# Storing the last unit of tokens before the third expert's weights are loaded, in a one-core cross-attention and mixture-of-experts kernel

## The reference

```python
x = x + xattn(layernorm(x), ctx, mask)          # tanh attention, then w_s * features + b_s
xn = layernorm(x)
probs = softmax(xn @ gate)                      # 4096 tokens, 8 experts
scores, token_idx = top_k(probs.T, k=512)
tok = xn[token_idx]
h = gelu(tok @ W1 + b1)
out_tok = h @ W2 + b2
routed = zeros.at[token_idx].add(out_tok * scores)
shared = gelu(xn @ Ws1 + bs1) @ Ws2 + bs2
x = x + routed + shared
```

## Time and profile before

| | us |
|---|---|
| median of 3 runs | 908.18 |
| lowest and highest run | 906.77, 911.2 |
| the profiled execution | 906.4 |
| its span in the profile | 904.6 |

### The profile page before, as it was taken

One profiled execution on the slowest core, in us unless ns is written; L12 is line 12 of the kernel. 1 busy time (PEld: TensorE's weight loads), 2 busy tenths in 40 slices (PEclk: granted clock), 3 DMA queues, 4 the chain that ended last, 5 costly groups with the idle time before them and its releaser, 6 DMA issues.

```text
span 904.6 us, 14092 instructions
## 1 busy us (share of the span) xinstructions
PE 802.1 (89%) x5355; PEld 471.2 (52%) x5355; DVE 710.8 (79%) x1412; ACT 767.4 (85%) x600; POOL 312.9 (35%) x563
## 2 busy tenths in 40 slices
PE   6865678579998999999999999999899899999995
PEld 4321123124443444445444464456676779999985
DVE  5799889897989699987979985976887577667640
ACT  4989999999999999999999999996653476676671
POOL 3301540705642008674004720070204134454423
PEclk9999999989999999999999999999999999999998
DMA  8000000000000000200000100003003345545512
GB/s 264 17 0 1 1 1 1 24 1 24 1 24 24 1 1 24 71 1 1 24 1 1 51 21 1 23 25 116 25 24 129 104 118 140 141 117 115 137 20 34
DMA packets 32405, 41.80 MB, mean 46 GB/s; under 512 B 2365, under 2 KB 29011, under 8 KB 32339
## 3 DMA queue, kind: packets, MB, share of 16 engines
q1 hardware_dynamic: 26083, 32.49, 10.9%
q0 software_dynamic: 6144, 8.39, 5.5%
q10 hardware_dynamic: 112, 0.04, 0.0%
HBM read 28.33 MB, written 12.58 MB: 45 GB/s over the span
## 4 chain that ended last, share of the span: by engine, by line
PE 38%; ACT 37%; issue 11%; DVE 9%; POOL 2%; DMA 1%; ACTq 0%; SPq 0%; DVEq 0%; POOLq 0%
ACT z L971 31%; PE bank L890 9%; PE bank L913 8%; PE bank L770 7%; PE bank L821 5%; DVE z L1329 4%; PE bank L806 3%; ACT z L967 2%; ACT u L1008 2%; PE bank L928 1%; PE bank L746 1%; PE bank L699 1%; DMA out_dram<-x_ring 1%; PE bank L864 1%; ACT L1008 1%
## 5 line engine op out<-in xcount | busy, mean ns | idle before, releaser
L971 ACT ACTIVATE z<-z 128x4096 f32<-128x4096 f32 (+5 forms) x157 | 521.1, 3365 | 6.2 <-DVE z L1329 6.0
L1329 DVE TENSOR_SCALAR z<-feat,txt_bias 128x1024 f32<-128x1024 f32 (+1 forms) x722 | 421.1, 654 | 34.6 <-PE bank L770 33.4
L770 PE MATMUL bank<-z,window 128*32 128x512 f32 x2464 | 307.2, 608 | 62.9 <-ACT z L971 61.4
L770 PEld LDWEIGHTS bank<-z,window 128*32 128x32 f32 x2464 | 70.1, 110 | 252.8 <-issue 136.0
L821 PE MATMUL bank<-ws_sb,u 128*128 128x256 f32 x512 | 128.1, 391 | 5.5 <-ACT u L1008 5.5
L821 PEld LDWEIGHTS bank<-ws_sb,u 128*128 128x128 f32 x512 | 93.2, 191 | 41.5 <-issue 19.8
L806 PE MATMUL bank<-tr,ws_s 128*128 128x512 f32 x384 | 107.4, 416 | 0.0
L890 PE MATMUL bank<-xg_s,w_s 128*128 128x512 f32 x384 | 101.0, 401 | 4.6 <-ACT hid L1044 4.4
L913 PEld LDWEIGHTS bank<-w_s,hid_s 128*128 128x128 f32 x672 | 86.4, 188 | 4.0
L913 PE MATMUL bank<-w_s,hid_s 128*128 128x256 f32 x672 | 88.2, 280 | 0.0
L806 PEld LDWEIGHTS bank<-tr,ws_s 128*128 128x128 f32 x384 | 69.5, 188 | 30.1 <-issue 16.4
(11 more groups left out here) (237 smaller groups left out, 750.9 us busy)
## 6 DMA issues: line engine op xcount, KB each, us to landing
w_raw<-in_L_ffn_W_dram SPq DMA_DIRECT2D x16, 1024.0 KB, 5.7
x_ring<-in_x_dram SPq DMA_DIRECT2D x8, 512.0 KB, 8.1
xn_dram<-xn SPq DMA_DIRECT2D x8, 512.0 KB, 2.9
out_dram<-x_ring SPq DMA_DIRECT2D x8, 512.0 KB, 2.9
u<-in_L_ffn_Ws_dram SPq DMA_DIRECT2D x1, 1024.0 KB, 11.2
ws_sb<-in_L_ffn_Ws_dram SPq DMA_DIRECT2D x1, 1024.0 KB, 13.6
xg<-xn_dram,idx POOLq DMA_INDIRECT x32, 4.0
out_dram<-y,idx POOLq DMA_INDIRECT x32, 3.9
```

What stands on the lines that cost most here:

```text
L770: ins = e.matmul(sums[v][32 * r:32 * r + 32, :], window[:, c, 31 - k:63 - k], z[:, n % ZB, at_piece:at_piece + TOK], start=(v, r) not in b ...
L971: e.activation(part, part, ACT.Tanh).then_inc(signal(*step), 1)
L1329: ins = e.tensor_scalar(z[:, n % ZB, i * width:(i + 1) * width], feat_of(units, c), bias_of(units, t, c), None, ALU.add)
```

## The change

Three settings change in the table of numbers at the top, and in `beside_experts` the place of the loads beside expert 0:

```diff
-EXPERT_FILL = (18, 5, 3)
+EXPERT_FILL = (20, 6, 0)
...
-LAST_END = 2
+LAST_END = 1
...
-        if ex + 2 < E and m in (1, 5):
-            steps.append(("load_w1" if m == 1 else "load_w2", ex + 2))
+        if ex + 2 < E and m in ((4, 7) if ex == 0 else (1, 5)):
+            steps.append(("load_w1" if m < 5 else "load_w2", ex + 2))
```

## The result

The changed kernel takes 900.81 us (median of 6 runs, 899.45 to 903.03), the kernel before 908.14 us (6 runs, 906.77 to 911.2). The ratio is 0.992, with a 95% interval from 0.9898 to 0.9942: 7.3 us faster, by the interval between 5.3 and 9.3 us. The profiled execution took 903.03 us, the slowest of the six, with a span of 901.3 us.

A forecast was written before the change was run, and what follows sets the result against it. The prediction took the late `x_ring` store, which stops ACT and then PE in expert 0, as the bound. 6.24 + 0.46 = 6.7 us off gave 899.7 us (profiled) or 901.5 us (median); forecast 901.0 us, range 898.8 to 903.8 us.

The forecast's parts named there:

- The wait and its cause: Expert 0: ACT's weight split waits 8.4 us for the `x_ring` store, held 7.6 us by its place in SP's queue.
- the distance: Time from expert 0's first `e_down` to expert 1's: 31.28 us before, 6.70 us longer than the next expert's 24.58 us.
- The sum, 6.24 + 0.46 = 6.7 us: Expert 0: 6.24 us for PE's stop plus 0.46 us for its list's wait on DVE's marking; bounds 6.2 and 8.2 us.
- 1.40 us of the 6.24 us are clock: After PE's 4.4 us idle, six matmuls took 2.93 us at half clock against 1.53 us at full clock.
- PE still had two slices in hand: At the store wait in expert 0, PE's loss is less than ACT's 8.4 us because two slices remained to work on.
- The down_end in a hole of DVE: Before slice 4's `e_lo`: the 1.28 us of `down_end` fill 0.96 us of DVE idleness, pushing `e_lo` some 0.3 us.
- EXPERT_FILL and the place of `load_w2` bring nothing: In expert 0: no shared-network matmul moves, and expert 2's `load_w2` still waits for the last `split_lo` of `w2`; no gain.
- The store's landing, 2.9 to 8.2 us, nearer to the first: SP's `x_ring` store, issued at about 705.6 us, lands at 708.5 us, at the worst 713.8 us.
- `load_w1` of expert 2 about 3 us early: SP's load lands at about 720.6 us, wanted by ACT's split in expert 1's slice 0 at 723.7 us: 3.1 us early.
- Rival D: Load of expert 2's `w1` becomes the new stop; slower from a 15.4 us landing, 912.8 us at 20 us; chance 0.02.
- rival B: POOL's gather of expert 2 takes the wait's place, 1.6 us late: gain 5.1 us, 903.1 us; chance 0.08.
- Rival C: At ACT's split, another awaited input is nearly as late: gain 0 to 1 us, 907 to 908 us; chance 0.05.

The follow-up runs named there:

- the loads moved alone: Kernel before with only expert 0's loads of expert 2's weights moved to slices 4 and 7, the two `down_end` staying in slice 2: ratio 0.9926.
- the early `down_end` alone: Kernel before with the two `down_end` in slice 1, the store still behind the load of `w1` of expert 2: ratio 0.9998.
- PE kept busy: Kernel before with 19 unused fp32 matmuls on PE before the `e_up` it stands still for: ratio 0.9974.
- LAST_END = 3: Changed kernel with the two `down_end` and the store moved to slice 3: ratio to the kernel before 0.9928.
- LAST_END = 1 alone: Kernel before with LAST_END set from 2 to 1, loads and EXPERT_FILL as before: ratio 0.9929.
- LAST_END = 4: Changed kernel with the two `down_end` behind the last `split_lo` of `w1`, the store still ahead of the load: ratio to the kernel before 0.9941.
- the store late in front: Loads at slices 4 and 7, LAST_END = 2, store ahead of the load but held for the same `split_lo`: ratio to the kernel before 0.994.

## Why the prediction was right, point by point

- *The wait and its cause.* Right. The store's place in SP's queue was all but 0.45 us of it: with the loads moved alone, which changes that place and no other order, the distance falls by 6.21 us; the early `down_end` alone gives no gain that can be timed.
- *The sum, 6.24 + 0.46 = 6.7 us.* The distance fell by 6.66 us, the two terms apart by 31.28 - 25.07 = 6.21 us and 0.45 us. The timed 7.3 us are 0.6 us more, inside the interval. Part of that may be the clock's cost in executions unlike the profiled one.
- *901.0 us, 898.8 to 903.8 us.* Measured 900.81 us. That the two agree to 0.2 us is luck. The sum on the median gives 901.5 us; the 0.5 us between came from setting the forecast between the profiled execution (899.7 us) and the median, a choice worth 1.8 us, for which nothing measured spoke. The changed kernel's own profiled execution was 2.2 us above its median.
- *1.40 us of the 6.24 us are clock.* Wrong, the step that failed. The matmuls did take 1.40 us longer than the 1.53 us they were held against (1.27 us longer than the 1.66 us of the same six with PE kept busy), but behind the stop PE had to wait for DVE's `split_lo` in any case; at full clock it waited 1.22 us there and lost the same. The sum did not hang on this step, because it was made with the distance and not with the parts. In a stop of this kind, the loss on PE is ACT's wait less what PE has in hand, which here was 8.4 - 6.2 = 2.2 us, which LAST_END = 3 and 4 confirm.
- *"PE still had two slices in hand".* Right, and now with a size, 2.2 to 2.3 us.
- *The down_end in a hole of DVE.* Right. In the changed kernel they run at 707.49 us and the `e_lo` follows at once; the list's 32 matmuls are one group again:

```profile
707.49 1.28 DVE L1486 TENSOR_TENSOR x_ring<-bank,x_ring 128x512 f32<-128x512 f32 x2
708.69 0.68 DVE L1637 TENSOR_TENSOR hid_s<-hid,hid_s 128x512 fp32r<-128x512 f32 x1
```

```profile
714.90 0.70 PE L864 MATMUL bank<-onehot,pick 128*32 128x128 bf16 x32
...
732.97 1.04 PE L699 MATMUL bank<-ident,xg 128*128 128x128 f32 x8
```

- *EXPERT_FILL and the place of `load_w2` bring nothing.* Right by the order of the instructions, and LAST_END = 1 alone has the distance of the whole change.
- *The store's landing, 2.9 to 8.2 us, nearer to the first.* 2.9 us.
- *`load_w1` of expert 2 about 3 us early.* The load was issued at 718.26 us, landed in 4.9 us at 723.2 us, and its split began at 726.98 us: 3.8 us early. Rival D had no ground.
- *The gather, rival B.* The mechanism is there and too small. The first piece took 1.68 us in place of 0.94 us:

```profile
720.14 1.68 POOL L1224 DMA_INDIRECT xg<-xn_dram,idx  x1 [19.33 <-DVE score L1626]
722.12 0.94 POOL L1224 DMA_INDIRECT xg<-xn_dram,idx  x1 [0.30 <-issue]
723.37 1.17 POOL L1224 DMA_INDIRECT xg<-xn_dram,idx  x1 [0.30 <-issue]
724.84 1.01 POOL L1224 DMA_INDIRECT xg<-xn_dram,idx  x1 [0.30 <-ACT y L1062]
```

The four pieces lost 1.0 us together, where the bound was 3.3 us, and PE turned the tokens at 732.97 us without waiting. DVE beside them:

```profile
719.78 1.22 DVE L1651 TENSOR_TENSOR w_s<-w_raw,w_s 128x1024 fp32r<-128x1024 f32 x1
721.55 0.69 DVE L1637 TENSOR_TENSOR hid_s<-hid,hid_s 128x512 fp32r<-128x512 f32 x1 [0.55 <-ACT hid_s L1054]
722.50 1.23 DVE L1651 TENSOR_TENSOR w_s<-w_raw,w_s 128x1024 fp32r<-128x1024 f32 x1 [0.26 <-ACT w_s L1029]
724.33 0.69 DVE L1637 TENSOR_TENSOR hid_s<-hid,hid_s 128x512 fp32r<-128x512 f32 x1 [0.61 <-ACT hid_s L1054]
```

The rule of the Trainium skill (SBUF — State Buffer, "Who interferes with whom") has the second to start blocked until the first is done. For POOL as the second the rows agree: DVE's instruction had still 0.86, 0.12, 0.36 and 0.18 us to run when the pieces started, and they took 0.74, 0, 0.23 and 0.07 us more than 0.94 us. For DVE as the second they do not: the `split_lo` at 722.50 us started 0.38 us after the second piece and took its usual 1.23 us. My bound had every piece meet a fresh `split_lo`, which they did not.
- *Rival C.* Nothing else was late at that split; with the store early, ACT goes into it without a wait.

## What to carry to other kernels

A one-off wait in a loop of equal bodies is best priced with the distance between bodies, not by adding up the slow instructions in it: what is slow inside a stop may be covered by the next wait. A queue that issues in program order holds back everything behind a wait, so a short transfer that somebody needs belongs in front of a load that is not free to go yet; and when both went at once here, the short one in front cost the load 1 us and saved the short one 5. When a piece of vector work is moved to make room, look at each instruction it now stands in front of, on its own engine.

## What the runs showed of the hardware that I had not expected

- A 512 KB store issued 0.46 us behind a 1 MB load on the same queue lands in 8.2 us, the load in 5.6 us; turned round, the store lands in 3.4 us and the load in 6.6 us; alone, the store takes 2.9 us. The order on one queue moves 4.8 us onto or off the small transfer for 1.0 us on the large one; gathers on POOL's queue were under way beside both pairs, and their part was not separated.
- After a stop of 4.4 us on PE the granted clock fell to 0.50 in both profiles that had one, but 1.1 us apart against the work and for different times: once 0.4 us ahead of the first matmuls, for 3.4 us, under another wait, at no cost; once 0.7 us behind their start, for 6.8 us, over the matmuls that set the pace, for 2.0 us. Idle stretches of 0.34 and 1.23 us with LAST_END = 4, and of 0.71 us with the store late in front, left it at 1.00.
